# Turning the chosen experts' inner activations by 32x32 blocks on VectorE and a round trip through DRAM instead of on TensorE, with the down product two groups later

## What is computed

```python
def _gemma_mlp(x, gate_w, up_w, down_w):          # H = 256, I = 1024
    g = jnp.einsum('bsh,hi->bsi', x, gate_w)
    u = jnp.einsum('bsh,hi->bsi', x, up_w)
    return jnp.einsum('bsi,ih->bsh', jax.nn.gelu(g, approximate=True) * u, down_w)
...
w, sel = jax.lax.top_k(softmax(router_logits), 2)
out = sum over the chosen e of w_e * _gemma_mlp(x, gate[e], up[e], down[e])
out = out + _gemma_mlp(x, shared_gate, shared_up, shared_down)
x = x + out
```

## Time and profile before

| | |
|---|---|
| median of 3 runs | 1191.1 us (1189.87 to 1192.92) |
| span of the profiled execution | 1190.3 us (its own time isn't recorded apart from that; it is 0.8 under the median) |
| TensorE busy | 1171.9 us, 98% |
| VectorE / ScalarE / GpSimd busy | 613.2 / 435.0 / 462.0 us |
| DMA moved | 177.88 MB, 149 GB/s mean |
| chosen groups | 170.5 to 776.5 us of the span |

### The profile page before, as it was taken

How to read it: one execution, slowest core, us unless ns; L and a number is a source line. 1 busy time by engine, 2 the same in 40 slices (tenths; PEclk the granted TensorE clock), 3 DMA queues, 4 the chain that set the end, 5 groups by cost and what they waited for, 6 DMA issues and landing times.

```text
span 1190.3 us, 25584 instructions
## 1 busy us (share of the span) xinstructions
PE 1171.9 (98%) x7406; PEld 1001.3 (84%) x7407; DVE 613.2 (52%) x1119; ACT 435.0 (37%) x845; POOL 462.0 (39%) x296
## 2 busy tenths in 40 slices
PE   8999999999999999999999999999999999899998
PEld 7999998788787888878788787889999999678876
DVE  6775775444444444454544454456555555434443
ACT  4355532222222322222222222222222232566664
POOL 3277688108145045180635481010000000888840
PEclk9999999999999999999999999999999999999999
DMA  7279866243253324352253531046644446578653
GB/s 209 63 252 327 286 203 222 67 134 99 68 172 107 126 64 138 100 184 84 83 157 114 183 88 50 18 140 176 182 134 132 132 131 241 169 223 244 212 151 117
DMA packets 159578, 177.88 MB, mean 149 GB/s; under 512 B 68480, under 2 KB 134272, under 8 KB 157440
## 3 DMA queue, kind: packets, MB, share of 16 engines
q1 hardware_dynamic: 145808, 126.83, 35.1%
q0 software_dynamic: 13680, 49.81, 13.7%
HBM read 143.04 MB, written 33.55 MB: 148 GB/s over the span
## 4 chain that ended last, share of the span: by engine, by line
PE 91%; DMA 3%; DVE 2%; POOL 1%; SPq 1%; issue 1%; ACT 1%; ACTq 0%; POOLq 0%; DVEq 0%
PE bank L713 14%; PE bank L714 14%; PE bank L715 14%; PE bank L802 9%; PE bank L1152 6%; PE bank L783 5%; PE bank L734 4%; PE bank L801 4%; PE bank L1181 3%; PE bank L995 2%; PE bank L853 2%; PE bank L1130 2%; PE bank L855 2%; PE bank L854 2%; PE bank L1161 1%; PE bank L804 1%
## 5 line engine op out<-in xcount | busy, mean ns | idle before, releaser
L559 POOL TENSOR_TENSOR W<-raw,one 128x1024 fp32r<-128x1024 f32 x79 | 150.2, 1901 | 565.7 <-DVE acc L1815 269.5
L1744 DVE TENSOR_TENSOR FS<-bank,FS 128x512 f32<-128x512 f32 (+1 forms) x200 | 133.7, 669 | 320.5 <-PE bank L715 276.3
L1242 ACT ACTIVATE FS<-bank 128x512 f32<-128x512 f32 (+1 forms) x200 | 116.1, 580 | 326.4 <-PE bank L715 299.7
L713 PE MATMUL bank<-W,RS 128*128 (+1 forms) x512 | 202.8, 396 | 1.9 <-DVE W L1856 1.9
L714 PE MATMUL bank<-W,RS 128*128 (+1 forms) x512 | 200.6, 392 | 0.0
L715 PE MATMUL bank<-W,RS 128*128 (+1 forms) x512 | 200.3, 391 | 0.0
L561 POOL TENSOR_TENSOR W<-raw,W 128x1024 fp32r<-128x1024 f32 x79 | 191.8, 2428 | 6.2
L802 PE MATMUL bank<-W,RS 128*128 x480 | 188.6, 416 | 0.0
L1252 ACT ACTIVATE RS<-bank 128x512 fp32r<-128x512 f32 x128 | 76.6, 598 | 152.1 <-PE bank L783 152.1
L713 PE MATMUL bank<-RS,W 128*128 128x256 f32 x448 | 129.1, 288 | 1.0 <-DVE RS L1734 1.0
L715 PE MATMUL bank<-RS,W 128*128 128x256 f32 x448 | 126.6, 283 | 0.0
(11 more groups left out here) (227 smaller groups left out, 2051.7 us busy)
## 6 DMA issues: line engine op xcount, KB each, us to landing
raw<-in_w POOLq DMA_DIRECT2D x87, 512.0 KB, 4.3
acc<-in_w SPq DMA_DIRECT2D x70, 512.0 KB, 4.7
mixes<-acc SPq DMA_DIRECT2D x16, 1024.0 KB, 6.3
W<-mixes SPq DMA_DIRECT2D x16, 1024.0 KB, 6.2
FS<-in_xT SPq DMA_DIRECT2D x200, 64.0 KB, 2.7
chosen_rows<-acc SPq DMA_DIRECT2D x64, 128.0 KB, 1.7
acc<-chosen_rows SPq DMA_DIRECT2D x128, 64.0 KB, 2.1
acc<-in_b SPq DMA_DIRECT2D x8, 640.0 KB, 10.9
```

Of the source, the lines that this page charges most:

```text
L559: pool.tensor_tensor(hi, raw[:, k, :], ones_like(PIECE), ALU.mult).then_inc(done, 1)
L713: pe.matmul(ps, ah, bh, start=(i == 0), stop=False)
L1242: act.activation(gl[h][:, 0:n], gate_ps[h][:, 0:n], ACT.Gelu_apprx_tanh).then_inc(gelu_done, 1)
L1744: TT(hid[h][:, 0:n], up_ps[h][:, 0:n], gl[h][:, 0:n], ALU.mult).then_inc(hid_done, 1)
```

## The change

The 512 turns of the chosen groups on TensorE go. In their place:

1. VectorE transposes `hid[h]` in 32x32 blocks (`hidden_squares`, one instruction per half) into `square[h]`.
2. SP writes `square[h]` to a DRAM buffer `squares[p]` (`write_squares`, two DMAs of 256 KB in 512-byte pieces), waits until both have landed, and reads it back with the blocks in their places (`read_hidT`, one DMA of 512 KB in 1-KB pieces) to the one tile `hidT`. A mixed group moves half as much.
3. ScalarE rounds from `hidT` in SBUF (`hidden_hi_chosen`), VectorE subtracts from `hidT` in SBUF (`hidden_lo_chosen`); both were read from PSUM before. The down weights are stored in the order of inner indices that this gives.
4. The down product runs two groups behind: in group s TensorE does up and gate of (s, 0), down of (s-2, 0), up and gate of (s, 1), down of (s-2, 1). The adds and stores, the release of weight slots, and the seam move with it; both halves' hi and lo of group s-1 are made at the end of group s.
5. In SP's queue the x loads, the writes, the store and the read take turns as the diff shows; the loads of bias rows move behind the chosen groups, since `hidT` lies where they are kept. `load_skill` of one place per round waits for an add. VectorE's wait for the spilled mixes stands before the first chosen group rather than the second.

```diff
+    squares = nc.dram_tensor("squares", (2, P, I0), F32, kind="Internal").ap()
...
-        hm = [acc[:, NSH + 25 + h, :] for h in range(2)]
+        hm = [acc[:, NSH + 31, :], routing[:, 5 * D:6 * D]]
+        square = [X1[:, :], acc[:, NSH + 25:NSH + 27, :].rearrange("p a d -> p (a d)")]
+        hidT = routing[:, 0:I0]
...
+        def turned_hid(h):
+            return hidT.rearrange("p (a h k t) -> p h k a t", a=4, h=2, k=4)[:, h]
...
+            def write_squares(s, p, at):
+                n = D if at.half is None else P
+                for h in range(2):
+                    sp.wait_ge(squared, 2 * s + h + 1)
+                    sp.dma_start(squares[p].rearrange("p (g y) -> p g y", g=4)[:, :, n // 2 * h:n // 2 * (h + 1)],
+                                 square[h][:, 0:2 * n].rearrange("p (g x) -> p g x", g=4)).then_inc(squares_out, 16)
+
+            def read_hidT(s, p, at):
+                n = D if at.half is None else P
+                if isinstance(s, int):
+                    sp.wait_ge(hl_done, 2 * (S0 + s))
+                sp.wait_ge(squares_out, 32 * s + 32)
+                sp.dma_start(hidT.rearrange("p (a y) -> p a y", a=4)[:, :, 0:n],
+                             squares[p].rearrange("(a i) (g y) -> (i g) a y", a=4, g=4)[:, :, 0:n])\
+                    .then_inc(hidT_in, 16)
...
+                for k in range(BODY):
+                    s, at = 2 + BODY * m + k, place_at(m, k - 2)
+                    if at.half != 0:
+                        load_skill(S0 + s + 2, k % 2, place_at(m, k + 2))
+                    if k < 2:
+                        load_mixed0(m, 0, ((0, 1, 2, 3), (4, 5))[k], S0 + BODY * m)
+                    if k in (HALVES[0] + 3, HALVES[0] + 4):
+                        load_mixed0(m, 1, ((0, 1, 2, 3), (4, 5))[k - HALVES[0] - 3], S0 + BODY * m + HALVES[0] + 3)
+                    write_squares(s, k % 2, place_at(m, k))
+                    if at.half != 0:
+                        store_chosen(S0 + s - 2, k % 2, at)
+                    else:
+                        load_skill(S0 + s + 2, k % 2, place_at(m, k + 2), added=S0 + s - 1)
+                    read_hidT(s, k % 2, place_at(m, k))
...
+            load_late(0)
+            write_squares(NR0 - 2, 0, LAST_TWO[0])
+            store_chosen(S1 - 4, 0, place(NR0 - 4))
+            read_hidT(NR0 - 2, 0, LAST_TWO[0])
+            write_squares(NR0 - 1, 1, LAST_TWO[1])
+            store_chosen(S1 - 3, 1, place(NR0 - 3))
+            read_hidT(NR0 - 1, 1, LAST_TWO[1])
+            load_late(1)
             for dst, src in ((b12, b1), (b2s, b2)):
...
+            def chosen_group(s):                       # TensorE
+                g, p, at, before = S0 + s, s % 2, place(s), None
+                e = load_expert_at(s)
                 for h in range(2):
                     if at.half is None:
                         up_gate(g, p, h, e, 2 * g + h, xset=1)
                     else:
                         up_gate_mixed(g, at, h)
-                    if h == 0:
-                        turn(1, 2 * g - 1, chunks=4 if before_at.half is None else 2)
...
-                    else:
-                        turn(0, 2 * g, chunks=4 if at.half is None else 2)
-                    before_down(h, before)
+                    if s == 0:
+                        down_shared(g - 2, 2 + h)
+                    elif s > 1:
+                        if h == 0:
+                            before = load_expert_at(s - 2)
+                        down_chosen(s - 2, h, before)
...
+            for q in range(2):
+                up_gate_late(0, 0, q)
+                last = load_expert_at(NR0 - 2 + q)
+                for h in range(2):
+                    down_chosen(NR0 - 2 + q, h, last)
...
+            def hidden_hi_chosen(s, h, at):            # ScalarE
+                act.wait_ge(hidT_in, 16 * s + 16)
+                act.wait_ge(down_done, 2 * (S0 + s) + h - 1)
+                if at.half is None:
+                    act.activation(by_chunk(hh[h]), turned_hid(h), ACT.Copy).then_inc(hh_done, 1)
...
                 gelu(1, 2 * g + 1, n=n)
-                hidden_hi(0, 2 * g, skipped=TURNLESS, mixed=mixed)
+                if before_at is not None:
+                    for h in range(2):
+                        hidden_hi_chosen(s - 1, h, before_at)
...
+            def hidden_squares(s, h, at):              # VectorE
+                n = 512 if at.half is None else D
+                dve.wait_ge(hid_done, 2 * (S0 + s) + h + 1)
+                if not (isinstance(s, int) and s == 0):
+                    dve.wait_ge(squares_out, 32 * s)
+                dve.transpose(square[h][:, 0:n], hid[h][:, 0:n]).then_inc(squared, 1)
+
+            def hidden_lo_chosen(s, h, at):
+                dve.wait_ge(hh_done, 2 * (S0 + s) + h + 1)
+                if at.half is None:
+                    TT(by_chunk(hl[h]), turned_hid(h), by_chunk(hh[h].bitcast(F32)), ALU.subtract).then_inc(hl_done, 1)
+                else:
+                    dve.tensor_copy(hm[h][:, P:D].rearrange("p (a t) -> p a t", a=4), turned_mixed(h, 1))\
+                        .then_inc(hl_done, 1)
...
+                g = S0 + s                             # chosen_group of VectorE
+                hidden_chosen(s, 0, at)
+                if before_at is None:
+                    hidden_lo_shared(1, 2 * g - 1)
+                hidden_squares(s, 0, at)
...
+                    split_x(g + 1, 1 - p, mixed=after_at.half is not None)
+                hidden_chosen(s, 1, at)
+                hidden_squares(s, 1, at)
...
                 for h in range(2):
+                    hidden_lo_chosen(s - 1, h, before_at)
+                if add_at is not None:
+                    add(g - 2, p, add_at)
```

233 lines of the change are left out of this document (118 added, 115 removed).

## The result

The changed kernel takes 1281.5 us (median of 4 runs, 1279.3 to 1283.1) where the kernel before takes 1191.2 (1189.9 to 1192.9): ratio 1.076, 95% interval 1.074 to 1.078. It is slower by 90 us; I had forecast 1185 with a range up to 1220. The turns did go (in the changed kernel TensorE has 512 matmuls fewer, and line 836, which was line 783, counts 32). What came in their place costs far more than they did.

What follows compares the result with a forecast made beforehand. TensorE, busy 98% of the span, was taken as the bound. Span 1190.3 - 57 + 32 + 10 + 2 + 2 + 5 = 1184.3, forecast time 1185 us, 8-in-10 range 1150 to 1220.

Steps and rivals of the forecast that it cites:

- -57 for the turns: TensorE, chosen groups: 512 of 544 turns go, at 0.111 us each, taking 57 us off the time.
- Block turns at 0.69: VectorE, two block transposes per full group: 0.69 us each, hidden behind TensorE.
- The read at 3.7: SP's 512 KB read of the turned tile: lands in 3.7 us, bounds 3.0 and 4.7.
- The write at 2.2: SP's writes of the turned blocks: land 2.2 us after issue, before the read may be issued.
- +32 for GpSimd's bursts: Eight bursts of GpSimd's weight splitting: low halves wait for GpSimd, loop 1.3 us over TensorE's, 32 us in all.
- +10 for the mixed groups: SP's queue: mixed weights just ahead of the writes make reads about 3 us late, +10 us (0 to 25).
- 3 us late does no harm: x loads behind SP's wait for the writes: issued 3.8 us into a group, needed by ScalarE at 10.5.
- none of the three is last: Waits of SP, ScalarE and VectorE: what is queued behind them isn't last while the landing is under 2 us late.
- The loop of 7.5 us against 8.28: Single landing tile, landing to next landing: 7.5 us against a full group's 8.28, 0.8 us to spare.
- Seam and start, +7: Both ends of the chosen groups: start +2 us (0 to 4), end +5 us (2 to 9).
- The rival on the slow side (C): Read lands in 4.5 us or more, TensorE waits for the low half in each group: 1215 to 1242; chance 0.28.
- the forecast itself (A): Stalls in GpSimd's bursts, none when quiet: 1185 us, from 1174 to 1198; chance 0.45.

Runs made afterwards that it cites:

- the roomier arrangement: Changed kernel with down halves behind both up halves, high and low parts a group later, two landing tiles, four DRAM buffers, pieces two a group: 1265.5 us; order mended, PSUM: 1227.1.
- e4_two_tiles: Changed kernel with a second landing tile for the turned activations and the read issued right behind its group's writes: 1269.6 us.
- the spread pieces alone: Changed kernel with the mixed expert pair's six weight pieces sent two per group behind the read, in three groups: 1248.2 us.
- e23_slack_queue_spread: Mended roomier arrangement, low halves from PSUM, mixed weights on ScalarE's queue, one piece per group (two in a single group): 1192.9 us, ratio 1.002 to the kernel before.

## Where the forecast was right and where it failed

The sum of the runs, in the order in which one thing after the other is added (in another order the parts would differ somewhat; the changed kernel with its own queue gives 37 where this ladder gives 44):

| kernel | us | step |
|---|---|---|
| before | 1191 | |
| turns on VectorE, no trip | 1144.7 | -47 |
| + the trip as traffic, mixed weights on their own queue | 1173.5 | +29 |
| + mixed weights back in SyncE's queue | 1217.2 | +44 |
| + everybody waits for the trip (the changed kernel) | 1281.5 | +64 |

Point by point:

- **-57 for the turns: right.** TensorE's busy time without the trip is 52 us lower at a clock of 0.996, and the span 49 lower.
- **Block turns at 0.69: right,** 0.711 in the median and 0.716 at most, also in GpSimd's bursts. The Trainium skill (SBUF - State Buffer, section SBUF: two separate sides) ties the lock to two-port modes or two SBUF inputs; the turn has one input, and the trace agrees: it never waited for GpSimd.
- **The read at 3.7: right** (median 3.9). The rule that the prediction quotes from the Trainium skill (DMA: Bandwidth & Descriptors, section Anatomy of one DMA) gives 3.2 as an estimate; it is fitted there to transfers issued by GpSimd, while this read is SyncE's. **The write at 2.2: wrong,** 3.5 in the median, 2.7 where neither GpSimd's loads nor mixed weights are near and 5.9 behind mixed weights. I had scaled from the 128 KB store in 128 pieces, but a write has 512 pieces of 512 B. A quiet group covers it; where it is late, VectorE's next block turn waits for it.
- **+32 for GpSimd's bursts: the mechanism was there, the term too small.** TensorE is idle for 45 us in them, and for 40 where the mixed weights are thin, and the lower clock comes on top. The low half takes 1.96 us there, where my working had about 1.6. I had put 0.3 us on GpSimd's loads sharing the DMA engines, but a write lands in 3.5 us there against 2.7 elsewhere and a read in 4.4 against 3.9 (medians, the ones right behind mixed weights left out). The lock is only a part of that: taking it away gives 16 us in the changed kernel (net of the further copy), 11 in the roomier arrangement, and it costs under 8 when there is no trip.
- **+10 for the mixed groups: the term that failed most clearly.** Taking the bursts' bytes away gives 45 us, moving them to another queue 37 to 44. My working was that the read is issued 2.9 us late; the queue made the write 7.1 us instead of 3.5, and SyncE, blocked on that landing, sent neither read nor x.
- **"3 us late does no harm" for x, and "none of the three is last": wrong.** I had named the instructions behind SyncE's and ScalarE's waits, but not VectorE's own wait, ahead of the block turn, for the writes of the group before, with the split of x queued behind it. The row at 532.40 is that wait. In a quiet group 0.2 to 1 us is to spare there.
- **The loop of 7.5 us against 8.28: too narrow a view.** I had priced the landing tile's loop; it is worth 12 us (e4_two_tiles). The binding path is longer: turn, write, read, high, low, down, with 1.8 us to spare when quiet and its three transfers in one queue.
- **The bytes: not priced at all.** I had compared mean rates (127 on top of 112 GB/s) with a burst's rate and concluded that it fits. The mean does. Where 1 or 2 MB of weights, GpSimd's pieces and the trip meet in one group it doesn't: share 1.00 and 1.07 of the 16 engines in the 5 us shown above. Bytes and SyncE's own waits together are 29 us.
- **The clock: not priced.** Some 35 us of the loss are TensorE's own work at the lower level behind the longer gaps.
- **Weights a group later, 0: right.** GpSimd's refills didn't come last. **Seam and start, +7:** within the 8 us of the kernel without the trip; not separated further.
- The rival on the slow side (C) had a trip too slow in every group. That isn't what happened: quiet groups are covered. Its time, 1242 at the most, fell short too. The signs of the forecast itself (A) were half there: the stalls in GpSimd's bursts came, but more than half of the idle time lies outside them, most of it behind mixed weights.

Taken together, the forecast had 51 us for all that is added (32 + 10 + 2 + 2 + 5), where 144 came (1277.7 of span against 1190.3 - 57). The late write was passed on by a wait of VectorE that the prediction did not list, GpSimd's loads and the mixed weights held up the transfers more than the two terms allowed, and the clock fell in the gaps.

What stays open: the 64 us of the last step are put down to the trip's latency met without slack. The roomier arrangement with the low halves from PSUM bears that out (1227 where the spread pieces alone gave 1248, and 1193 with the queue and thinner bursts), but how they divide between write, read and lock was not measured one by one. Nor did any run take GpSimd's weight loads away, in whose bursts most of what was left stands; how much of that is its share of the DMA engines and how much the longer low half is not shown. Whether e23_slack_queue_spread can be brought under the kernel before was not tried further.

## What to carry to other kernels

A transfer put into a loop has to be priced on the path from its producer to its user, with the landing of everything that stands ahead of it in its queue, and each engine's wait for it listed with what is queued behind. Here a quiet pass had under 2 us to spare, and the bursts of two other streams of loads became idle time of the bound engine, to which the lower clock behind long gaps added. Bulk loads belong on another queue than small transfers that are waited for, and spread so that no single pass asks more of the DMA engines than it has time for. When one link of a chain of waits is taken out and the time stays, look where the same microseconds come up next: here the up product's 49 us of gaps came up at the down product, and the two together stayed 83 to 87.

## What the runs showed of the hardware that I had not expected

- A 256 KB write in 512 B pieces landed in 3.5 us in the median, and one in 7.1 behind 2 MB in the same queue; with the weights on another queue the median was 3.1, and VectorE's wait for it fell from 95 to 9.5 us.
- On a queue of its own a 512 KB read still took 8.3 us when 1 MB from ScalarE's queue and GpSimd's 512 KB pieces met it, with the engines' share at 1.07 and 345 GB/s.
- In the 5 us that hold the end of a gap of 7.3 us (526.54 to 533.82) the granted clock was 0.50, then 0.57 over 5 us of full work, and back at 1.00 in the 5 us after that; over the whole kernel the mean fell from 1.000 to 0.965, worth some 35 us of TensorE's time.
- A subtraction with two operands in SBUF took 0.68 us on average outside GpSimd's bursts and 1.96 in them, at most 2.9; with one operand in PSUM it took 0.69 at most in both, and a block turn never over 0.72.
